# A recommendation model's attention kernel: embedding rows by one-hot matmul in float32r instead of bf16, one position more

## What is computed

```python
seq_embed  = concat([emb_seq[i][seq_inputs[:, :, i]] for i in range(2)], -1)      # 2048 x 40 x 128
item_embed = concat([emb_seq[i][item_inputs[:, i]] for i in range(2)], -1)        # 2048 x 128
q    = broadcast(item_embed)
info = concat([q, seq_embed, q - seq_embed, q * seq_embed], -1)
h    = sigmoid(info @ att_W1 + att_b1)            # 512 -> 80
h    = sigmoid(h @ att_W2 + att_b2)               # 80 -> 40
att  = softmax(where(mask, h @ att_Wf + att_bf, NEG_INF))
user_info = einsum('bl,bld->bd', att, seq_embed)
x    = batchnorm(concat([user_info, item_embed, dense, sparse_embeds], -1))
x    = prelu(x @ ffn_W1 + ffn_b1); x = prelu(x @ ffn_W2 + ffn_b2); out = sigmoid(x @ out_W + out_b)
```

## Time and profile before

| | |
|---|---|
| median of 3 runs | 1768.76 us (1767.96 to 1770.26) |
| profiled execution: its own time | 1768.3 us |
| its span, first to last instruction | 1766.4 us |
| busy, share of the span | PE 82%, POOL 73%, DVE 42%, ACT 27% |
| weight loads (PEld) | 46% |
| granted TensorE clock, mean | 0.904 of full speed |
| gathers (POOL's queue) | 41.50 MB, 14.3% of 16 DMA engines |

### The profile page before, as it was taken

The page is one execution under the profiler, slowest core; times in us unless marked ns, Lnnn a source line. Parts: engine busy times, 40 slices in busy tenths (PEclk is TensorE's granted clock), DMA queues, the critical chain, the costliest instruction groups (busy, mean ns, idle before and its releaser), DMA issues.

```text
span 1766.4 us, 23414 instructions
## 1 busy us (share of the span) xinstructions
PE 1451.0 (82%) x7602; PEld 804.7 (46%) x7602; DVE 745.5 (42%) x2217; ACT 475.1 (27%) x813; POOL 1295.3 (73%) x1269
## 2 busy tenths in 40 slices
PE   0098896979789796979969797897969799797978
PEld 0054453535445453545535353554535355453532
DVE  3534434353533535353443534344353534435343
ACT  2323223131322213132231323222232312322133
POOL 6877777777777777777777777777777777777710
PEclk9999897989889897998979898898979999798985
DMA  6411111121111112111111211111121111112200
GB/s 132 115 25 44 26 29 41 25 44 26 43 27 28 42 25 45 26 43 26 44 27 25 44 26 43 27 43 26 26 45 26 43 26 43 27 25 44 26 5 0
DMA packets 58900, 64.25 MB, mean 36 GB/s; under 512 B 33351, under 2 KB 33683, under 8 KB 58263
## 3 DMA queue, kind: packets, MB, share of 16 engines
q0 software_dynamic: 40448, 41.50, 14.3%
q1 hardware_dynamic: 17474, 14.55, 2.9%
q10 hardware_dynamic: 850, 6.50, 1.5%
HBM read 62.36 MB, written 0.11 MB: 35 GB/s over the span
## 4 chain that ended last, share of the span: by engine, by line
PE 79%; DVE 8%; ACT 5%; issue 5%; DMA 1%; SPq 1%; DVEq 0%; ACTq 0%
PE grown L416 45%; PE pre L429 8%; PE pre L431 8%; PE pre L438 5%; PE turned L401 5%; PE small L445 4%; DVE sums L910 2%; ACT stage L621 2%; DVE stage L849 1%; ACT hist_t L611 1%; DMA stage<-in_L_rec_emb_seq_dram 1%; PE small L505 1%; SPq L297 1%; ACT x L592 1%; PE small L455 1%
## 5 line engine op out<-in xcount | busy, mean ns | idle before, releaser
L337 POOL DMA_INDIRECT hist<-in_L_rec_emb_seq_dram,idx x1184 | 1213.1, 1025 | 360.8 <-issue 336.1
L416 PE MATMUL grown<-stage,split 128*128 128x384 bf16 x4704 | 838.5, 331 | 0.0
L416 PEld LDWEIGHTS grown<-stage,split 128*128 128x128 bf16 x4704 | 459.7, 99 | 389.2 <-issue 127.1
L832 DVE TENSOR_TENSOR prod_t<-turned,item_t 128x512 f32<-128x512 f32 x160 | 110.7, 692 | 447.8 <-ACT hist_t L611 447.8
L849 DVE TENSOR_SCALAR stage<-rel 128x768 bf16<-128x768 bf16 x784 | 237.6, 362 | 20.3 <-issue 20.1
L616 ACT ACTIVATE hidden<-pre 80x512 f32<-80x512 f32 x160 | 94.7, 592 | 556.2 <-DVE pre L840 556.2
L840 DVE TENSOR_TENSOR pre<-pre,item_part 80x512 f32<-80x512 f32 x160 | 111.0, 694 | 282.2 <-PE pre L431 282.2
L429 PE MATMUL pre<-hist_t,w_hist 128*80 128x512 f32 x320 | 168.5, 608 | 29.9 <-ACT hist_t L611 29.9
L431 PE MATMUL pre<-prod_t,w_raw 128*80 128x512 f32 x320 | 170.5, 616 | 0.0
L910 DVE SCALAR_TENSOR_TENSOR sums<-hist,weight,sums 128x128 f32<-128x128 f32 x576 | 160.9, 343 | 0.5
L611 ACT COPY hist_t<-turned 128x512 f32<-128x512 f32 x160 | 93.6, 585 | 227.2 <-PE turned L401 226.9
(11 more groups left out here) (119 smaller groups left out, 627.6 us busy)
## 6 DMA issues: line engine op xcount, KB each, us to landing
hist<-in_L_rec_emb_seq_dram,idx POOLq DMA_INDIRECT x1184, 2.5
keys<-key_rows SPq DMA_DIRECT2D x34, 384.0 KB, 3.9
stage<-in_L_rec_emb_seq_dram ACTq DMA_DIRECT2D x4, 1372.0 KB
sparse_rows<-in_L_rec_emb_sparse_dram,idx_sparse POOLq DMA_INDIRECT x48, 3.3
stage<-in_L_rec_emb_seq_dram ACTq DMA_DIRECT2D x4, 183.8 KB
raw<-in_r_seq_inputs_dram SPq DMA_DIRECT2D x1, 600.0 KB, 17.1
items<-in_L_rec_emb_seq_dram,idx POOLq DMA_INDIRECT x32, 3.6
w_raw<-in_L_rec_att_W_dram SPq DMA_DIRECT2D x1, 160.0 KB
```

The costliest lines, as they stand in the source:

```text
L337: gp.indirect_dma_start(rows, None, table, bass.IndirectOffsetOnAxis(ap=index, axis=0)).then_inc(landed, 16)
L416: last = nc.tensor.matmul(grown[n][:, 0:MC], split[n][:, c, k, :], hot[:, slot, n * MC:(n + 1) * MC], start=(c == 0 and k == 0), stop=(c = ...
```

## The change

- MP goes from 3 to 4: all of group 9 comes from TensorE. POOL gathers 74 times a tile. `hist` holds 36 positions, and the rows turned back go to `last_rows`, from which the last `add_group` reads.
- The tables are two float32r parts, `high` (ACT's copy to float32r, which rounds) and `low` (the remainder, one DVE subtraction). A chunk is four matmuls of 512 columns. A table row pair (even and odd row) takes the place of the two half tables, so the key is row // 2 and the half is its last bit.
- The tables come in eight pieces of 12 or 13 chunks through two slots, laid into `hist[:, 1]`; the issue of piece q+1 stands behind the copy of piece q in ACT's program, and behind the subtraction of piece q-1.
- The keys stay float32 and are compared with `lane_key[:, c]` (49 x partition + c); `relate` goes. The source has three runs of 342 at a pitch of 344, the destination is one run of 1026; the last two columns are not used. `hot` has seven slots.
- SP loads the keys of a tile once the tile before has turned group 9, and the halves (bf16) once its user vector is ready.
- The accumulators of the weighted sum lie in PSUM. `pre2` and the logits share one bank; PE waits for `softmax_step` before layer 2 of group 7.
- `sparse_rows` lies in `hist[:, 0]`, and the sparse gathers wait until tile 14 is consumed; `picked` lies in the keys, `last_rows` in the halves.

Its core, as a diff:

```diff
-    MP = 3
+    MP = 4
-    SPLITS = 3
-    HOTS = 14
+    HOTS = 7
...
-        split = [sb(f"split{n}", [P, CH, SPLITS, 2 * E], BF16) for n in range(NB)]
+        high = [sb(f"high{n}", [P, CH, 2 * E], F32R) for n in range(NB)]
+        low = [sb(f"low{n}", [P, CH, 2 * E], F32R) for n in range(NB)]
+        PIECES = [(0, 13), (13, 25), (25, 37), (37, CH)]
+        PIECE = 13 * 2 * E
+        staged = [hist[:, 1, k * PIECE:(k + 1) * PIECE].rearrange("p (c e) -> p c e", e=2 * E) for k in range(2)]
+        RB = 3
+        RC = -(-NB * MC // RB)
+        hot = sb("hot", [P, HOTS, RB * RC], F32R)
+        keys = sb("keys", [P, RB, RC + 2])
...
+            with sp.Fori(1, TILES) as tile:
+                wait(sp, group_turned, tile * GROUPS)
+                load_keys(tile)
+                wait(sp, user_ready, tile)
+                load_uppers(tile)
...
-                                for k in range(SPLITS):
-                                    last = nc.tensor.matmul(grown[n][:, 0:MC], split[n][:, c, k, :],
-                                                            hot[:, slot, n * MC:(n + 1) * MC],
-                                                            start=(c == 0 and k == 0), stop=(c == CH - 1 and k == SPLITS - 1))
+                                wanted = hot[:, c % HOTS, n * MC:(n + 1) * MC]
+                                nc.tensor.matmul(grown[n][:, 0:MC], high[n][:, c, :], wanted, start=(c == 0), stop=False)
+                                last = nc.tensor.matmul(grown[n][:, 0:MC], low[n][:, c, :], wanted, start=False,
+                                                        stop=(c == CH - 1))
...
+            for q in range(NB * len(PIECES)):
+                n, (first, end), k = q // len(PIECES), PIECES[q % len(PIECES)], q % 2
+                landed[k] += 16 * (3 if first < SHORT else 2)
+                act.wait_ge(table_landed[k], landed[k])
+                nc.scalar.copy(high[n][:, first:end, :], staged[k][:, 0:end - first, :]).then_inc(high_ready, 1)
+                if 0 < q < NB * len(PIECES) - 1:
+                    act.wait_ge(low_ready, q)
+                    load_piece(q + 1)
...
-                            last = nc.vector.tensor_scalar(hot[:, slot, :], rel[half][:, :], float(c), None, ALU.is_equal)
-                            last.then_inc(hot_ready, 1)
+                            nc.vector.tensor_scalar(hot[:, c % HOTS, :], keys[:, :, 0:RC], lane_key[:, c:c + 1], None,
+                                                    ALU.is_equal).then_inc(hot_ready, 1)
...
-                    heat(0, 9)
+                    heat(0, 7)
                     row_numbers(tile + 1, 1 - half)
...
-                        heat(PER * g + 6, PER * g + 9)
+                        heat(PER * g + 3, PER * g + 7)
                         add_item(g, g % 2)
-                        heat(PER * g + 9, PER * g + 12)
+                        heat(PER * g + 7, PER * g + 9)
                     add_item(EARLY - 1, 0)
-                    heat(PER * EARLY, CH)
+                    heat(PER * (EARLY - 1) + 3, CH)
```

More of the change, by code:

```diff
@@ L23 @@
 I32 = mybir.dt.int32
+F32R = mybir.dt.float32r
 BF16 = mybir.dt.bfloat16
@@ L55, in build @@
     MK = MP * NB
+    KEYS = TILES * MK
     VH = V // 2
@@ L162, in build @@
         inv_total = sb("inv_total", [P, 1])
-        early_sum, odd_sum, user = (pool[:, spare + N // 2 + i * D:spare + N // 2 + (i + 1) * D] for i in range(3))
+        early_sum = sb("early_sum", [P, D])
+        odd_sum = sb("odd_sum", [P, D])
+        user = sb("user", [P, D])
         x = sb("x", [P, 3, P])
-        sums = sb("sums", [P, 2, D])
         part = sb("part", [H1, ROWS])
@@ L405, in turn_group @@
                             for n in range(NB):
-                                last = nc.tensor.matmul(turned[g % 2][n * E:(n + 1) * E, P:N], fold[:, :], picked[:, n, :],
+                                last = nc.tensor.matmul(turned[g % 2][n * E:(n + 1) * E, TURNED * P:N], fold[:, :], picked[:, n, :],
                                                         start=True, stop=True)
@@ L640, in _ @@
                         sigmoid1(g, g % 2)
-                    act.wait_ge(keys_landed[1 - half], 32 * (pair + (1 + half)))
-                    act.wait_ge(rel_used, tile + 1)
-                    relate(1 - half).then_inc(rel_ready, 1)
                     sigmoid2(EARLY - 3)
@@ L704, in _ @@
         def _(dve):
-            dve.sem_inc(rel_used, 1)
-            for slot in range(2):
-                last = nc.vector.memset(stage[3 * P // 4:P, slot, SHORT * E:CH * E], 0.0)
-            last.then_inc(stage_cleared, 1)
+            for k in range(2):
+                last = nc.vector.memset(staged[k][3 * P // 4:P, :, :], 0.0)
+            last.then_inc(table_cleared, 1)
             nc.vector.memset(w2[:, :], 0.0)
@@ new lines, in _ @@
+            nc.vector.tensor_scalar(pair_of, row, 1, None, ALU.arith_shift_right)
+            key_done(nc.vector.tensor_scalar(odd_of, row, 1, None, ALU.bitwise_and))
+            for k, of in ((0, pair_of), (1, odd_of)):
+                for t in range(TILES):
+                    last = nc.vector.tensor_copy(by_table[k][:, t, :, :], of[:, t, :].rearrange("p (j n) -> p j n", n=NB))
+            last.then_inc(keys_ready, 1)
+            for q in range(NB * len(PIECES)):
+                n, (first, end), k = q // len(PIECES), PIECES[q % len(PIECES)], q % 2
+                dve.wait_ge(high_ready, q + 1)
+                nc.vector.tensor_tensor(low[n][:, first:end, :], staged[k][:, 0:end - first, :], high[n][:, first:end, :],
+                                        ALU.subtract).then_inc(low_ready, 1)
```

243 lines of the change are left out of this document (104 added, 139 removed).

## The result

The changed kernel takes **1896.25 us** (median of four runs, 1895.37 to 1897.06), the kernel before beside it 1769.03: 1.072 times as long (95% interval 1.070 to 1.074), 7.2% slower. The forecast was 1830, and its range ended at 1895, so the time lies just outside it. The sign was right, the size was half: 127 us came, 61 were forecast.

The account below looks back on a forecast made before the run. PE was taken as the bound, POOL a close second. Per tile -5.5 + 5.3 + 3.1 + 0.4 = +3.3; sixteen tiles 53 and setup 8 took the span from 1766.4 to 1827, forecast 1830 us, range 1745 to 1895.

Parts of the forecast that it names:

- What bounds: Kernel before: PE paces at 102.2 us a tile, with POOL a close second at 99.9.
- Part 1: PE's table matmuls: four float32r matmuls of 512 columns a chunk, starting every 216 ns; -5.5 us a tile.
- rival C: PE's float32 weight loads are not hidden behind the matmul before: matmuls of 0.32 us, 2116 us in all; chance 0.06.
- D: PE's matmuls take two cycles a column: 0.43 us each, 2451 us in all; chance 0.04.
- Part 2: DVE's compare of 1026 float32 elements runs at plain pace: 1,230 ns, starting every 1.14 us against 0.267.
- (a): Tile start: seven plain compares ahead of row_numbers and dense_now, for which PE waits; +5.3 us a tile.
- (b): Groups 1 to 5: DVE's 8.06 us of work fits within PE's 8.36; cost 0.
- My sign for the contrary: Groups over 8.6 us apart, with DVE's waits in groups 1 to 5 gone, would mean DVE paces there.
- (c): Tail: ten compares after the last early add_item delay the product PE wants for group 7; +3.1 us a tile.
- Part 3: Fourth position: bigger picks, wider fold matmuls, one more transpose in the turn back; +0.4 us a tile.
- Part 4: POOL: two gathers fewer a tile, 92.5 us, and no stretched gathers; 0 gained, since PE paces.
- Part 5: Setup: table pieces of some 850 KB, one load in flight, last subtraction at 86.0; +8 us (3 to 11).

Follow-up runs that it names:

- e4: The changed kernel with three positions from TensorE instead of four (384 columns a matmul, 76 gathers): 1642.92 us, 0.928 of the kernel before.
- e3: The changed kernel with contiguous keys, so a compare reads one even run instead of three: 1807.99 us, 1.022 of the kernel before.
- e9: The changed kernel with both table parts and the one-hots in bf16 instead of float32r: 1842.36 us, 1.042 of the kernel before.
- e1: The changed kernel with dense_now and row_numbers moved ahead of the tile's first compares: 1761.24 us, 0.9954 of the kernel before.
- e6: The changed kernel with only the first 256 columns of each bank multiplied in chunks 1 to 47: 1785.79 us, one run.
- e10: The changed kernel with a tile's last four compares cut to 342 of 1026 elements: 1850.29 us, 46 us less than the changed kernel.

## Why the prediction was right in sign and half in size

- **What bounds.** PE paces and POOL is close behind: right. Where a matmul and a compare had fewer columns (e4) or the compare was fast (e3), POOL paced at once.
- **Part 1, -5.5 a tile: the step that failed.** "I take 216": rivals C and D (0.32, 0.43) are out, so a float32r operand streams in one pass, as argued, but its columns take 0.457 ns, not 0.417. From group 0 to group 6, 36 chunks gave 1.1 us, 0.031 a chunk instead of 0.112: -1.5 a tile. (Four steps of 0.233 would give 0.043; the 0.09 a group behind layer 2, see e9, takes 0.015 of it.) In bf16 (e9) the same 36 gave 3.9, 0.109 each, so the formula was right for the type whose rows I had, and I had no row of the other. This one term is 4.0 of the missing 5.3 us a tile. The range kept only 216 for the forecast case and jumped to 0.32 in rival C; between them it had nothing, and that is where the value lay.
- **Part 2, the compare.** 1.19 instead of 1.14 a start. With 768 elements at 0.920 the slope is 1.043 ns an element, as taken. One compare lasted 1,271 ns and not 1,230, so the fixed part was 0.04 more, and the overlap 0.08, not 0.09. The Trainium skill (VectorE: DVE Perf Modes, What auto-detection actually checks) held in all four shapes run here: three runs against one, 1026 or 768, went plain (1.19, 0.92); one run against one, 1024 or 342, went fast (0.66, 0.31).
- **(a), +5.3:** right. User turn to dense_now grew by 5.9, and e1 took it away.
- **(b), 0:** right. PE paced the groups and DVE kept waiting. My sign for the contrary, groups over 8.6 apart, would have misled alone: 8.85 came from PE's matmuls. DVE's own pace is 8.33 (e6).
- **(c), +3.1:** right. The two waits are 2.6. From group 6 to group 8 the tile grew by 2.7 though 11 chunks got shorter, so 3.0 in all, and e10 took the wait for the product away. With the faster bf16 matmul (e9) PE arrives earlier, and the two waits are 3.2 (17.7 and 34.0 over 16), as I had reckoned for that matmul; in three tiles of four the clock then falls behind the wait, and three to seven matmuls start 0.43 us apart.
- **Part 3, +0.4:** not there. At the full clock the two stretches behind group 8 take 4.49 and 12.08 us with four positions (e1, e9), and 4.53 and 12.05 before. The sums in PSUM cost nothing, 349 ns against 343.
- **The clock: not in the sum.** At the tile's start the first seven matmuls lie 0.43 us apart, the 1.2 GHz level, in nearly every tile: 1.5 us lost. Before, four or five lay 0.32 apart in one tile and nine to eleven in the next: 1.2 lost, so +0.3. Layer 1 of group 8 falls to the lower clock in every one of these tiles, where before it did in every second: group 8 to group 9 takes 5.35 instead of 4.86, +0.5. From group 9 to the user turn it is 12.44 instead of 12.05, +0.4. Together +1.2 a tile, some 19 us. Ahead of the second place PE had stood still for 1.56 us (until 376.47), then worked until 384.23 with waits of 0.57 and 0.68; but e1 has the same waits and no fall at group 8, so what decides it isn't shown.
- **Part 4, POOL 0:** right in size, wrong in where it waits: for DVE's row numbers, 17 us a tile (244.6 in 14).
- **Part 5, +8: wrong sign, -7.** I had taken a piece for some 850 KB beside loads of 1,562; eight pieces of the same tables are 781 each, which by the first load gives 6.4 us, and six of 6.4 came. But the issue of a load starts together with the copy I had put ahead of it (both at 34.71), so five copies of 1.5 fell out of my chain, and it began at 29.0, not 36.2; why the first copy could start at 25.5 and not at 31.7 I did not trace. Together 15 us in the other direction. That was luck: it hid part of Part 1's error, and with my +8 the time would have been some 1911 us.
- **The sum as measured:** -1.5 + 5.9 + 3.0 + 0 + 1.2 = 8.6 a tile, as in the trace. Against the forecast that is 4.0 in Part 1, 0.6 in (a), -0.1 in (c), -0.4 in Part 3 and 1.2 in the clock: the 5.3 that were missing. Sixteen of 8.6 are 138, and 7 less in the setup 131, against 127 in the span (1893.3 less 1766.4).

## What to carry to other kernels

A price that no row shows needs a range that is continuous up to the next rival: eight percent on an instruction that runs 3,136 times was 54 us. Ask of a bigger tile what the extra elements buy and on which engine: the fourth position cost PE 12 and DVE 13 us a tile to spare POOL 2.5. And a producer whose output another engine wants at once must stand ahead of the long run of work, not behind it: moving one small copy and five small steps was worth 135 us. And where two kernels are compared stretch by stretch, look at the granted clock of each stretch before its length is put down to the change.

## What the runs showed of the hardware

- A float32r matmul streams a column in 0.45 to 0.46 ns with scatter (0.224 to 0.237 for 512), bf16 in 0.42 almost without; the width of its weights does not matter (0.232 with 64 columns). The Trainium skill (FP8 and Floating Point Precision, TensorE Precision Notes) gives four passes for true FP32, which agrees with the float32 rows (860 ns for 512 columns, four times 216), and for reduced-precision FP32 only that it is truncated, without a rate.
- Weight loads of 194 ns in the same rows lie behind matmuls that are 234 ns apart, shortening them to 141 changed nothing, and in e6 the matmuls came every 119 ns with loads of 207. The Trainium skill (TensorE: Matmul & The Clock Gate, Part 3, The mechanism) says in one sentence that a load overlaps only where the row groups differ, which the runs contradict, and in another that it is also pulled ahead when it goes to the background weight buffer, which they would allow.
- Compares that take two elements at a time stretch POOL's gathers: 49 of 0.75 us cost it 15.5 us a tile (e3), 49 of 0.36 had cost 4.9 (before), and plain ones none: in the changed kernel and in e4 no gather of tiles 1 to 14 lasts over 1.02 us. A gather that meets a row of them waits for the whole row (7.48 us beside ten).
